# Attention passes: two of a chunk's sixteen gathered columns picked by one-hot fp32 products from a table in SBUF

## The chip, the cores and the metric

The kernel runs on one core of one Trainium2 chip. The metric is the device time of one execution in microseconds, the median of the runs shown.

## What is computed

The reference runs three graph attention layers and one edge MLP over 12,500 nodes with 32 features and 400,000 edges. The edges are sorted by their destination `dst`; `src` is random.

```
def _gat(x, edge_index, W, att_s, att_d, bias, heads, ch, neg_slope):
    h = (x @ W.T).reshape(n, heads, ch)
    a_s = (h * att_s[None]).sum(-1);  a_d = (h * att_d[None]).sum(-1)
    logits = leaky_relu(a_s[src] + a_d[dst], neg_slope)
    m = segment_max(logits, dst);  ex = exp(logits - m[dst])
    denom = segment_sum(ex, dst);  alpha = ex / (denom[dst] + 1e-16)
    return segment_sum(alpha[:, :, None] * h[src], dst).reshape(n, heads * ch) + bias
x = layernorm(x + three_gat_layers(x))
e = relu(concat(x[src], x[dst], edge_attr) @ W1 + b1) @ W2 + b2
x = layernorm(x + maximum(segment_max(e, dst), x))
```

All of it is fp32. The costly part is `h[src]`: for each edge of each layer a row of 32 numbers is fetched from a table of 12,500 rows.

## The kernel before

**Work and tiling.** The 400,000 edges are cut into four quarters of 100,000, and each quarter into 196 chunks of 512 edges (the last two have 352 and 320). A chunk holds 4 x 512 = 2048 edges, laid out as 128 partitions by 16 columns. A pass runs over all 196 chunks. There are three attention passes and one MLP pass, and a node step before each that turns the sums of the pass before into new node features.

**Gathering.** The node step writes `h` for all nodes to `table` in HBM (12,544 rows of 32). For each chunk POOL issues sixteen indirect DMAs, one for each column, in `gather_edges` (L589). Each fetches one row of 32 numbers for each of the 128 partitions, at the indices in `idx`, into a 32-number slot of `g`. There are four `g` and four `idx` buffers, used in turn. The ACT refills `idx` for the chunk four ahead (`refill`) once DVE has read `g`. In the MLP pass the same code fetches rows of 64 numbers from `tablex`.

**One chunk of an attention pass.** DVE's `turn` (L1255) waits for the sixteen gathers and transposes `g` in blocks of 32x32 into `h_sb`, features on the partitions and edges along the free axis. `lead` then scans the destinations' terms forward along the edges (`adf`, L1265). TensorE's `front` computes a restart row (`p_r`, bf16, 4 rows, L676) and spreads the destinations' terms over the partitions (`p_ad`, two fp32 products with 4 rows, L692); `source` makes the attention term of the sources from `h_sb` (`p_as`, L701). DVE's `logits` (L1274 to L1285) forms the logits and their running maximum, ACT's `exps` (L864, L865) the exponentials, and DVE's `sums` (L1292 to L1302) the running sums, which are transposed back and stored to `state` by ACT.

**What sets the order.** Each engine's order is written out by hand. DVE runs `logits(k)`, `lead(k+1)`, `sums(k)`. TensorE runs `front(k)`, `source(k-1)`. ACT runs `exps(k)`, `refill(k+1)`, `restart(k+2)`, `ends_in(k)`, `sloped(k+1)`, `ends_out(k)`. SP loads `ad` and `r_in` two chunks ahead (`load_gat`). POOL issues gathers in chunk order and waits only for `idx`. Semaphores tie them: `tin` counts DVE's transposes, `adf` its scans, `pas` the source products, `e_g` the gathers that landed, `aidx` the index tiles.

**The MLP pass** does two fp32 products of 128 rows on the edge features (L729) and two on the hidden layer (L735), two Relus with a bias column on ACT (L936), and gathers in the same way. `xd_in` holds its destination rows; no attention pass touches it.

Of the kernel before, what the change touches and what calls it, by code (L numbers as in the profile page):

```python
# [19 lines left out]
HID = 64  # L20
# [34 lines left out]
ROUND = float(3 * 2 ** 22)  # L55

# [13 lines left out]
def build(nc, I, out):  # L70
# [3 lines left out]
    with ctx:  # L74
# [11 lines left out]
        def view(t, offset, dims, parts=P, p0=0):  # L86
# [16 lines left out]
        vmax = dram("vmax", (EP, F), fp32)  # L103

# [37 lines left out]
        dt_ = sb("dt_", [HALF, 8, L + 1], i32)  # L142
        rbf = sb("rbf", [HALF, 8, L], bf16)
        row_id = sb("row_id", [P, SAMPLES], i32)
        nodebuf = sb("nodebuf", [P, 2 * TU * L])
# [39 lines left out]
        xd_in = [sb(f"xd_in{b}", [P, W, HID]) for b in range(2)]  # L185
# [3 lines left out]
        hid = d_b  # L189

# [28 lines left out]
        sel_p = [view((xd_in + [dm_t])[t // 8], t % 8 * P, [[1, P]]) for t in range(KT)]  # L219
# [9 lines left out]
        p_t, p_n = bank[0], bank[1:5]  # L229
        p_start, p_next = bank[5][:, 0:NT], bank[5][0:P - 1, P:P + 2]  # L230
# [6 lines left out]
            "l1", "rowi", "bound", "cntv", "sel", "acc", "start", "wpe", "ticks2", "tickl")}  # L237
# [4 lines left out]
            "d", "ph", "s", "ts", "td", "tm", "dm", "st0", "st1")}  # L242
# [41 lines left out]

        def quarters(rows, v):
# [15 lines left out]
        def _(eng):  # L301
# [7 lines left out]
            eng.dma_start(row_id[:, :], I["row_first"].partition_broadcast(P)).then_inc(S["d0"], 16)  # L309

# [71 lines left out]

            head = [eng.value_load(dstp.rearrange("(a b) -> a b", b=1)[LEAD + q * Q:LEAD + q * Q + 1, :], min_val=0, max_val=NP - 1) for q in range(NQ)]
# [3 lines left out]
            def node(step):  # L387
# [24 lines left out]
                if step == 0:  # L412
                    fill_aux()
                    later_inputs()
                    eng.wait_ge(S["rw"], 1)
                    for k in range(8):
                        at = (k % 2) * HALF * NQ * L + (k // 2) * L
                        n = min(HALF, NF - (k % 2) * HALF)
                        eng.dma_start(bass.AP(tensor=rrow.tensor, offset=at, ap=[[NQ * L, n], [1, L]]), rbf[0:n, k, :]).then_inc(S["rw"], 16)
                    for v, at, f, l, n in pieces:  # L420
                        eng.dma_start(bass.AP(tensor=rrow.tensor, offset=v * NQ * L + at, ap=[[NQ * L, 1], [L, NQ], [1, n]]),
                                      view(rbf, L + l, [[2 * L, NQ], [1, n]], parts=1, p0=f - HALF)).then_inc(S["rw"], 16)
                for u in range(NN):
                    eng.wait_ge(n_s[u], (step + 1) * TN * 16)
                for b in range(2):
                    eng.wait_ge(D[f"tst{b}"], TST[b][step + 1])
# [5 lines left out]
            for layer in range(3):  # L432
                node(layer)
                if layer == 0:
                    eng.wait_ge(S["rw"], 1 + 16 * (8 + len(pieces)))
                load_gat(layer, 0, 0)
                load_gat(layer, 1, 1)

                def steps(v, b):
                    if not isinstance(v, int) or v + 2 < NC:  # L440
                        load_gat(layer, v + 2, b)
# [9 lines left out]
                def both(i):  # L451
                    steps(i * 2, 0)
                    steps(i * 2 + 1, 1)
                    fill_x(i)
                both(0)
                with eng.Fori(1, NC // 2 - 2) as i:
                    both(i)
                both(NC // 2 - 2)
                both(NC // 2 - 1)
            node(3)  # L460

            def load_mlp(v, b):
                need(eng, M["pre"], v * 2 - 2)
                tick(eng, "tickl")
                load_r(v, b, M[f"ld{b}"])
                eng.dma_start(chunk_tile(xd_in[b], v, HID), chunk_rows(auxx, v)).then_inc(M[f"ld{b}"], 16)
# [37 lines left out]
        def _(eng):  # L504
            eng.memset(ident[:, :], 0.0).then_inc(S["blk"], 1)
            for o, pattern, base, mult in ((riota, [[BLK, SAMPLES]], 0, 0), (kid_last[:, :], [[BLK * P, KT]], BLK - 1, BLK),
                                           (blk_odd[:, :], [[2 * BLK, NBLK]], -1, 2 * BLK * NBLK), (j_half[:, :], [[1, BLK]], 0, 0),
                                           (kid[:, :], [[P, KT]], 0, 1), (miota[:, :], [[1, P]], 0, 0), (nid[:, :], [[1, NT]], 0, NT)):
# [73 lines left out]
            def gather_edges(pass_, n, k, count=W):  # L582
# [4 lines left out]
                for j in range(count):  # L587
# [24 lines left out]
        def gathered(pass_, i, k, h):  # L612

            last = min(W // 2, max(0, cols(NI - 1, k) // SQ - h * (W // 2))) * 16
            before = pass_ * ((NI - 1) * (W // 2 * 16) + last)
            return before + (NI - 1) * (W // 2 * 16) + last if type(i) is int and i == NI - 1 else i * (W // 2 * 16) + before + W // 2 * 16
# [3 lines left out]
        def _(eng):  # L620
# [57 lines left out]
            for layer in range(3):  # L678
# [23 lines left out]

                front(0, 0)
                front(0, 1)
                source(0, 0)
                for k in range(2, NB):
                    front(0, k)
                    source(0, k - 1)
                with eng.Fori(1, NI - 1) as i:
# [4 lines left out]
                source(NI - 2, NB - 1)  # L714
                for k in range(1, NB):
                    source(NI - 1, k - 1)
                    front(NI - 1, k)
                source(NI - 1, NB - 1)
# [33 lines left out]
        def _(eng):  # L752
# [89 lines left out]
            for layer in range(3):  # L842
# [48 lines left out]

                def chunk(i, k):
                    exps(i, k)
                    if layer or type(i) is not int or i * NB + k > 0:
# [4 lines left out]
                    ends_out(i, k)  # L899
                if layer == 0:  # L900
# [12 lines left out]
                for k in range(NB - 1):  # L913
                    exps(NI - 1, k)
                    ends_in(NI - 1, k)
# [51 lines left out]
        def _(eng):  # L967
# [151 lines left out]
            last.then_inc(S["rw"], 1)  # L1119
            eng.wait_ge(S["par"], N_PAR * 16)  # L1120
# [124 lines left out]
            for layer in range(3):  # L1245
# [3 lines left out]

                def turn(i, k):  # L1250
                    b = k % 2
                    for h in range(2):
# [51 lines left out]
                def chunk(i, k):  # L1304
                    logits(i, k)
                    lead(i if k + 1 < NB else i + 1, (k + 1) % NB)
                    sums(i, k)
                if layer == 0:
                    turn(0, 0)
                    turn(0, 1)  # L1310
# [6 lines left out]
                for k in range(NB - 1):  # L1317
                    logits(NI - 1, k)
                    sums(NI - 1, k)
# [113 lines left out]
```

## Time and profile before

| | |
|---|---|
| median of 3 runs | 16743.22 us (16742.36 to 16745.18) |
| span of the profiled execution | 16709.0 us |
| median of the runs less that span | 34.2 us |
| POOL busy | 12580.8 us (75%) |
| DVE busy | 9733.0 us (58%) |
| TensorE busy (matmul) | 5230.6 us (31%) |
| ACT busy | 2187.6 us (13%) |

The profile shows one execution and gives its span, from the first to the last instruction; a run's time is measured around it, and what lies between the two is launch and end. Busy time is the time in which an engine worked on instructions that the profile counts. A share says little by itself: an engine that starts its next instruction as soon as it can is the bound at 75% too, if the rest is its own issuing.

### The profile page before, as it was taken

How to read it: one execution, taken by the hardware profiler on the slowest of the kernel's cores; microseconds unless marked ns; L12 is line 12 of the kernel's file. 1: busy time of each engine (PE TensorE's matmuls, PEld its weight loads, DVE VectorE, ACT ScalarE, POOL GpSimd, SP SyncE). 2: the span in 40 equal slices, each digit the busy share in tenths (PEclk: the TensorE clock that was granted, in tenths of full speed). 3: DMA queues.
4: the chain of work that ended last, by engine and by line, in shares of the span. 5: the costliest groups of instructions: out<-in, count | busy, mean ns of one | idle time of the engine just before them, and what ended most of it. 6: DMA issues, size and time to landing. Idle time of an engine off the chain costs nothing. (4 is left out here: it accounts for less than half of the span.)

```text
span 16709.0 us, 72365 instructions
## 1 busy us (share of the span) xinstructions
PE 5230.6 (31%) x6238; PEld 1537.5 (9%) x6238; DVE 9733.0 (58%) x11755; ACT 2187.6 (13%) x4747; POOL 12580.8 (75%) x13328
## 2 busy tenths in 40 slices
PE   2333333332233333333223333333323333333332
PEld 1000000000000000000000000000000111111110
DVE  6666666666466666666546666666664444444445
ACT  2111111111011111111101111111111111111110
POOL 7777777777777777777777777777777777777777
PEclk9999999999999999999999999999995666666665
DMA  2111111111011111111101111111112222222222
GB/s 77 58 55 55 56 55 57 55 58 48 20 29 29 29 29 29 29 29 29 28 20 29 29 29 29 28 29 29 29 34 71 79 79 79 79 79 79 79 79 56
DMA packets 639804, 794.40 MB, mean 48 GB/s; under 512 B 252774, under 2 KB 418460, under 8 KB 627084
## 3 DMA queue, kind: packets, MB, share of 16 engines
q0 software_dynamic: 426768, 272.89, 8.8%
q1 hardware_dynamic: 99804, 295.38, 4.8%
q10 hardware_dynamic: 113184, 225.69, 3.7%
q14 instruction: 42, 0.34, 0.0%
q8 instruction: 6, 0.10, 0.0%
HBM read 442.63 MB, written 350.37 MB: 47 GB/s over the span
## 5 line engine op out<-in xcount | busy, mean ns | idle before, releaser
L589 POOL DMA_INDIRECT g<-table,idx x9375 | 8846.2, 944 | 2859.0 <-issue 2856.7
L692 PE MATMUL bank<-ad,ad_sel 4*128 4x512 f32 (+1 forms) x2352 | 2211.4, 1088 | 5306.7 <-DVE adf L1265 5306.7
L589 POOL DMA_INDIRECT g<-tablex,idx x3125 | 2948.4, 943 | 952.4 <-issue 952.4
L1255 DVE STREAM_TRANSPOSE h_sb<-g 128x512 f32<-128x512 f32 (+1 forms) x588 | 606.6, 1032 | 4002.1 <-DMA g<-table,idx 4002.1
L735 PE MATMUL bank<-d_b,w_out 128*128 128x512 f32 (+1 forms) x784 | 727.6, 1083 | 2462.0 <-ACT d_b L936 2462.0
L676 PE MATMUL bank<-r_in,qsel 4*128 4x512 bf16 (+2 forms) x784 | 444.0, 566 | 2875.9 <-issue 1841.0
L1352 DVE STREAM_TRANSPOSE bank<-g 128x512 f32<-128x512 f32 x196 | 142.1, 725 | 1940.8 <-DMA g<-tablex,idx 1940.8
L701 PE MATMUL bank<-h_sb,w_as 128*128 128x512 f32 x1176 | 1216.7, 1139 | 137.5 <-DVE h_sb L1255 137.5
L692 PEld LDWEIGHTS bank<-ad,ad_sel 4*128 4x128 f32 x2352 | 676.0, 316 | 6220.5 <-DVE adf L1265 5603.3
L754 ACT ACTIVATE idx<-idx_all 128x16 int32 (+1 forms) x784 | 168.7, 216 | 6149.2 <-DVE h_sb L1255 3873.2
L1265 DVE TENSOR_TENSOR_SCAN adf<-r_sb,adf,bank 128x512 f32<-128x512 f32 (+1 forms) x588 | 710.2, 1208 | 113.8 <-PE bank L692 113.8
L1281 DVE TENSOR_TENSOR_SCAN mb<-r_sb,mb,xw 128x512 f32<-128x512 f32 (+1 forms) x588 | 751.3, 1278 | 20.7
L1296 DVE TENSOR_TENSOR_SCAN s_b<-pc,s_b,xw 128x512 f32<-128x512 f32 (+1 forms) x588 | 750.4, 1276 | 20.8
L1292 DVE TENSOR_TENSOR_SCAN d_b<-pc,d_b,xw 128x512 f32<-128x512 f32 (+1 forms) x588 | 728.2, 1238 | 12.1 <-ACT pc L865 12.1
L1285 DVE TENSOR_TENSOR xw<-xw,mb 128x1024 f32<-128x1024 f32 (+1 forms) x588 | 721.9, 1228 | 20.1
L754 ACT ACTIVATE r_sb<-bank 128x512 f32<-128x512 f32 (+2 forms) x784 | 466.7, 595 | 1547.2 <-DVE s_b L1360 1111.7
L864 ACT ACTIVATE xw<-xw 128x512 f32<-128x512 f32 (+1 forms) x588 | 341.3, 580 | 2387.1 <-DVE xw L1285 2387.1
L1278 DVE TENSOR_TENSOR xw<-u_sb,xw 128x512 f32<-128x512 f32 (+1 forms) x588 | 408.2, 694 | 355.9 <-ACT u_sb L872 355.9
L1298 DVE STREAM_TRANSPOSE dm_t<-d_b 128x512 f32<-128x512 f32 (+1 forms) x588 | 592.3, 1007 | 0.0
L754 ACT ACTIVATE o_sb<-dm_t 128x64 f32<-128x64 f32 (+1 forms) x588 | 181.5, 309 | 3076.5 <-DVE dm_t L1299 3076.5
L1302 DVE STREAM_TRANSPOSE o_sb<-s_b 128x512 f32<-128x512 f32 (+1 forms) x588 | 581.4, 989 | 0.0
L1299 DVE STREAM_TRANSPOSE dm_t<-mb 128x512 f32<-128x512 f32 (+1 forms) x588 | 580.1, 987 | 0.0
(225 smaller groups left out, 7127.5 us busy)
## 6 DMA issues: line engine op xcount, KB each, us to landing
state<-o_sb ACTq DMA_DIRECT2D x582, 288.0 KB, 2.1
g<-table,idx POOLq DMA_INDIRECT x9375, 2.3
auxx<-wide SPq DMA_DIRECT2D x97, 1056.0 KB, 4.2
xd_in<-auxx SPq DMA_DIRECT2D x194, 512.0 KB
xe_t<-in_edge_attr SPq DMA_DIRECT2D x196, 256.0 KB
g<-tablex,idx POOLq DMA_INDIRECT x3125, 2.4
vmax<-o_sb ACTq DMA_DIRECT2D x194, 256.0 KB, 2.1
r_in<-rrow SPq DMA_DIRECT2D x776, 4.0 KB
```

Of the source, the lines that this page charges most:

```text
L589: eng.indirect_dma_start(o, None, t[:, :], bass.IndirectOffsetOnAxis(ap=idx[k][:, j:j + 1], axis=0)).then_inc(e_g[k][j // (W // 2)], 16)
L692: last = eng.matmul(p_ad[:, 0:c], ad_sel[:, h, :], view(ad[b], h, [[2, c]], parts=NQ), start=(h == 0), stop=(h == 1))
L701: eng.matmul(p_as[:, 0:c], w_as[layer][:, :], h_sb[b][:, 0:c], start=True, stop=True).then_inc(E["pas"], 1)
L735: last = eng.matmul(p_v[:, 0:cols(v)], w_out[:, h, :], hid[h][:, 0:cols(v)], start=(h == 0), stop=(h == 1))
L754: return eng.activation(o, i, ACT.Copy)
L1255: v_.transpose(view(h_sb[b], 0, [[1, w], [w, SQ]]), view(g[k], 0, [[F, w], [1, F]])).then_inc(E["tin"], 1)
L1265: v_.tensor_tensor_scan(adf[b][:, 0:c], r_sb[b][:, 0:c], p_ad[:, 0:c], adf[1 - b][:, e - 1:e], ALU.min, ALU.max).then_inc(E["adf"], 1)
L1281: v_.tensor_tensor_scan(mb[b][:, 1:c + 1], r_sb[b][:, 0:c], xw[:, 0, 0:c], mb[b][:, 0:1], ALU.min, ALU.max).then_inc(E["mb"], 1)
L1285: v_.tensor_tensor(xw[:, :, 0:c], xw[:, :, 0:c], view(mb[b], 1, [[0, 2], [1, c]]), ALU.subtract).then_inc(E["dif"], 1)
L1292: v_.tensor_tensor_scan(d_b[b][:, 0:c], pc[:, 0:c], xw[:, 0, 0:c], d_b[1 - b][:, e - 1:e], ALU.mult, ALU.add).then_inc(E["d"], 1)
L1296: v_.tensor_tensor_scan(s_b[b][:, 0:c], pc[:, 0:c], xw[:, 0, 0:c], s_b[1 - b][:, e - 1:e], ALU.mult, ALU.add).then_inc(E["s"], 1)
L1298: v_.transpose(dm_t[:, 0, 0:w, :], view(d_b[b], 0, [[1, w], [w, SQ]])).then_inc(E["td"], 1)
```

## The change

In the attention passes, columns 0 and 1 of each chunk are no longer gathered (`SEL = 2`); columns 2 to 15 are. The MLP pass still gathers all sixteen.

Node `n` of the table is written as `n = 98 p + 14 b + t`, with partition `p` (the *key*, 0 to 127), block `b` (0 to 6) and place `t` (0 to 13). At the start of each pass SP loads the whole table into `h_all` (an idle part of `nodebuf`, 12,544 rows, node `98 p + s` on partition `p`), and ACT reorders it into `by_place`, seven blocks of 32 features by 14 places, 448 numbers for each partition. Once, at the start of the kernel, DVE splits the source index of the selected edges into `key = floor(n / 14)` (that is `7 p + b`), and `t` and `t * t` (`digits`), and SP writes them to HBM as `keys` and `digit`.

For each chunk and each pass:

- SP loads the chunk's 256 keys, broadcast to 128 partitions (`kb`, two buffers), and three rows of 256 (one, t, t squared; `ms`, four buffers).
- ACT makes seven one-hot matrices `oh` of 128x256 (one buffer): seven Squares of (key - own key), then one Relu of 1 - 2 x that over all 1792 columns.
- TensorE, for each of the two columns, adds into one PSUM bank of 128x448 (`p_sel`, banks 4 and 5) one product with 3 rows (`ms` by `mcoef`), which is zero at the wanted place and at most -2^118 elsewhere, and seven products with 128 rows (`oh` by `by_place`). All are fp32.
- DVE takes the maximum over the 14 places for each feature, which leaves the wanted row, and writes it into `g` where the gather used to.

The orders become: DVE `logits(k)`, `lead(k+1)`, `picked(k+2)`, `sums(k)`; TensorE `front(k)`, `source(k-1)`, `select(k+1)`; ACT `exps(k)`, `one_hot(k+3)`, then as before; SP `load_gat(k+2)`, `load_sel(k+3)`. Some tiles that are idle in the attention passes are shared (`oh` with `xd_in`, `by_place` and `ms` with the setup's tiles).

```diff
@@ gather_edges (POOL)
-                for j in range(count):
+                for j in range(SEL if pass_ < 3 else 0, count):
...
@@ block.sync
+            def load_sel(layer, x, k):
+                n = layer * NC + x
+                need(eng, E["far"], n - 1)
+                tick(eng, "tickl")
+                need(eng, E["sel"], n - 3)
...
+                eng.dma_start(kb[k % 2], row.partition_broadcast(P)).then_inc(E[f"lk{k % 2}"], 16)
+                eng.dma_start(ms[k], cols_).then_inc(E[f"lk{k % 2}"], 16)
...
+                    eng.dma_start(h_all, table.rearrange("(p t) c -> p (t c)", t=NT)).then_inc(E["href"], 16)
+                    for x in range(3):
+                        load_sel(step, x, x)
...
@@ block.tensor
+                def select(i, k):
+                    n = i * NB + (layer * NC + k)
+                    need(eng, E["oh"], n + 1)
+                    for c in range(SEL):
+                        at = slice(c * P, (c + 1) * P)
+                        need(eng, E["red"], n * SEL + (c + 1 - SEL))
+                        eng.matmul(p_sel[c][:, 0:FT], ms[k][:, at], mcoef[:, :], start=True, stop=False)
+                        for b in range(NN):
+                            last = eng.matmul(p_sel[c][:, 0:FT], oh[:, b, at], by_place[:, b, :], start=False, stop=(b == NN - 1))
+                    last.then_inc(E["sel"], 1)
...
                 with eng.Fori(1, NI - 1) as i:
                     for k in range(NB):
                         front(i, k)
                         source(i - (k == 0), (k - 1) % NB)
+                        select(i if k + 1 < NB else i + 1, (k + 1) % NB)
...
@@ block.scalar
+                def halves():
+                    eng.wait_ge(E["href"], (layer + 1) * 16)
+                    for b in range(NN):
+                        last = copy(by_place[:, b, :].rearrange("p (f t) -> p f t", f=F), view(nodebuf, b * FT, [[1, F], [F, TN]]))
+                    last.then_inc(E["by"], 1)
+
+                def one_hot(i, k):
+                    x = i * NB + k
+                    n = x + layer * NC
+                    need(eng, E[f"lk{k % 2}"], (x - k % 2) * 16 + (layer * NC * 16 + 32))
+                    tick(eng, "ticks")
+                    need(eng, E["oh"], n)
+                    tick(eng, "ticks")
+                    need(eng, E["sel"], n)
+                    for b in range(NN):
+                        last = eng.activation(oh[:, b, :], kb[k % 2], ACT.Square, scale=-1.0, bias=key_at[:, b:b + 1])
+                    last.then_inc(E["far"], 1)
+                    need(eng, E["far"], n + 1)
+                    eng.activation(oh[:, :, :], oh[:, :, :], ACT.Relu, scale=-2.0, bias=1.0).then_inc(E["oh"], 1)
+
                 def chunk(i, k):
                     exps(i, k)
+                    one_hot(i if k + 3 < NB else i + 1, (k + 3) % NB)
...
@@ block.vector
+                def picked(i, k):
+                    n = i * NB + (layer * NC + k)
+                    need(eng, E["sel"], n + 1)
+                    for c in range(SEL):
+                        v_.tensor_reduce(view(g[k], c * F, [[1, F]]), view(p_sel[c], 0, [[TN, F], [1, TN]]), AX.X, ALU.max).then_inc(E["red"], 1)
+
                 def turn(i, k):
                     b = k % 2
+                    n = i * NB + (layer * NC + k)
+                    need(eng, E["red"], n * SEL + SEL)
...
                 def chunk(i, k):
                     logits(i, k)
                     lead(i if k + 1 < NB else i + 1, (k + 1) % NB)
+                    picked(i if k + 2 < NB else i + 1, (k + 2) % NB)
                     sums(i, k)
```

## Rows read from the trace of the kernel before

**Rows 1.** The page: busy time by engine; granted clock in 40 slices, in tenths.

```profile
PE 5230.6 (31%) x6238; PEld 1537.5 (9%) x6238; DVE 9733.0 (58%) x11755; ACT 2187.6 (13%) x4747; POOL 12580.8 (75%) x13328
...
PEclk9999999999999999999999999999995666666665
```

**Rows 2.** The page, costliest groups: out<-in, count | busy, mean ns | idle, releaser.

```profile
L589 POOL DMA_INDIRECT g<-table,idx x9375 | 8846.2, 944 | 2859.0 <-issue 2856.7
...
L1255 DVE STREAM_TRANSPOSE h_sb<-g 128x512 f32<-128x512 f32 (+1 forms) x588 | 606.6, 1032 | 4002.1 <-DMA g<-table,idx 4002.1
```

**Rows 3.** Timeline of one attention chunk: start, duration, engine, line, operation [idle before].

```profile
2001.42 1.04 DVE L1255 STREAM_TRANSPOSE h_sb<-g 128x512 f32<-128x512 f32 x1 [6.63 <-DMA g<-table,idx]
...
2003.45 1.24 DVE L1292 TENSOR_TENSOR_SCAN d_b<-pc,d_b,xw 128x512 f32<-128x512 f32 x1
...
2003.58 3.78 PE L692 MATMUL bank<-ad,ad_sel 4*128 4x512 f32 x4 [9.34 <-DVE adf L1265]
...
2007.29 2.08 PE L701 MATMUL bank<-h_sb,w_as 128*128 128x512 f32 x2
...
2009.43 0.67 DVE L1274 TENSOR_TENSOR xw<-adf,bank 128x512 f32<-128x512 f32 x1
...
2013.54 1.23 DVE L1285 TENSOR_TENSOR xw<-xw,mb 128x1024 f32<-128x1024 f32 x1
...
2014.80 0.58 ACT L864 ACTIVATE xw<-xw 128x512 f32<-128x512 f32 x1 [4.07 <-DVE xw L1285]
...
2015.29 0.59 ACT L865 ACTIVATE pc<-xw 128x512 f32<-128x512 f32 x1
...
2021.42 1.04 DVE L1255 STREAM_TRANSPOSE h_sb<-g 128x512 f32<-128x512 f32 x1 [6.65 <-DMA g<-table,idx]
```

**Rows 4.** Timeline of TensorE, two chunks of the MLP pass, and one weight load.

```profile
12704.46 3.78 PE L735 MATMUL bank<-d_b,w_out 128*128 128x512 f32 x4 [12.89 <-ACT d_b L936]
...
12709.02 1.98 PE L729 MATMUL bank<-xe_t,w_hid 128*128 128x512 f32 x4 [0.27 <-DVE pc L1342]
12709.61 0.19 PEld L729 LDWEIGHTS bank<-xe_t,w_hid 128*128 128x128 f32 x1 [0.30 <-DVE mb L1342]
...
12724.35 3.78 PE L735 MATMUL bank<-d_b,w_out 128*128 128x512 f32 x4 [13.35 <-ACT d_b L936]
...
12728.91 3.75 PE L729 MATMUL bank<-xe_t,w_hid 128*128 128x512 f32 x4 [0.25 <-DVE pc L1342]
```

**Rows 5.** Windows in these chunks: stretch, length, busy by engine, granted clock, DMA, GB/s.

```profile
12708.00:12709.00 1.00, 0.75 (x2) 0.10 (x1) 1.00 (x3) 0.00 (x0) 0.95 (x1) 0.70 0.17 33
12709.00:12710.00 1.00, 0.98 (x3) 0.50 (x4) 1.00 (x2) 0.00 (x0) 0.72 (x1) 1.00 0.14 33
...
12715.00:12716.00 1.00, 0.00 (x0) 0.00 (x0) 0.00 (x0) 0.00 (x0) 0.69 (x2) 0.71 0.05 10
...
12732.50:12733.00 0.50, 0.16 (x1) 0.00 (x0) 0.00 (x0) 0.00 (x0) 0.20 (x1) 1.00 0.97 393
...
12735.50:12736.00 0.50, 0.00 (x0) 0.00 (x0) 0.00 (x0) 0.00 (x0) 0.50 (x1) 0.91 0.09 29
```

**Rows 6.** Timeline of ACT in the MLP pass.

```profile
13023.25 0.69 ACT L936 ACTIVATE d_b<-bank,b_hid 128x512 f32<-128x512 f32 x1 [0.26 <-DVE bank L1356]
13023.85 0.69 ACT L936 ACTIVATE d_b<-xw,b_hid 128x512 f32<-128x512 f32 x1
```

**Rows 7.** Groups by line and shape: Sign, table load and reduction (last of the third node step).

```profile
L764 ACT ACTIVATE x_nm<-nodebuf,bound 128x512 f32<-128x512 int32 x49 | 35.4, 722 | 1.6
...
L764 ACT ACTIVATE x_nm<-row_id,blk_odd 128x784 f32<-128x784 int32 x14 | 13.3, 949 | 0.4
...
L822 ACT ACT_TABLE_LOAD x7 | 9.0, 1283 | 0.1
...
L1235 DVE TENSOR_REDUCE row<-nodebuf 128x14 f32<-128x448 f32 x7 | 4.3, 620 | 0.2
```

**Rows 8.** The page, DMA issues: out<-in, engine, count, KB, us to landing.

```profile
auxx<-wide SPq DMA_DIRECT2D x97, 1056.0 KB, 4.2
```

More of the change, by code:

```diff
@@ L55 @@
 ROUND = float(3 * 2 ** 22)
+SEL = 2
+FT = F * TN
+SPLIT = NT * F
+FAR = float(2 ** 118)
+NKEY = NC * SEL
 def first(v):
@@ L103, in build @@
         vmax = dram("vmax", (EP, F), fp32)
+        keys = dram("keys", (NC, SEL * P), fp32)
+        digit = dram("digit", (3, NC * SEL * P), fp32)
         ident = sb("ident", [P, P])
@@ L184, in build @@
         gx = g
-        xd_in = [sb(f"xd_in{b}", [P, W, HID]) for b in range(2)]
+        xd2 = sb("xd2", [P, 2, W, HID])
+        xd_in = [xd2[:, b, :, :] for b in range(2)]
         xds = [[adf[b], h_sb[b]] for b in range(2)]
@@ L189, in build @@
         hid = d_b
+        oh = view(xd2, 0, [[SEL * P, NN], [1, SEL * P]])
+        h_all = nodebuf[:, 0:NT * F]
+        src_key = mb[0][:, 0:NKEY].bitcast(i32)
+        key = xe_t[0][:, 0:NKEY]
+        digits = [xe_t[1][:, 0:NKEY], view(x1_nm, 0, [[1, NKEY]])]
+        ones = view(o_sb[0], 0, [[1, NKEY]])
+        place14 = view(o_sb[1], 0, [[1, FT]], parts=3)
+        place_sq = view(o_sb[0], 0, [[1, FT]], parts=3)
+        place_c = view(o_sb[1], FT, [[1, 1]], parts=3)
         ends = sb("ends", [P, 3, OW])
@@ L449, in fill_x, with four @@
                                       wide[:, 0:min(w, total - i * w) if isinstance(i, int) else w]).then_inc(S["wide"], 16)
[L451 to L459, printed above, removed]
+                def four(i):
+                    for k in range(NB):
+                        steps(i * NB + k, k)
+                        if k % 2:
+                            fill_x(i * 2 + k // 2)
+                four(0)
+                with eng.Fori(1, NI - 1) as i:
+                    four(i)
+                four(NI - 1)
             node(3)
@@ L612, in gathered @@
         def gathered(pass_, i, k, h):
-            last = min(W // 2, max(0, cols(NI - 1, k) // SQ - h * (W // 2))) * 16
-            before = pass_ * ((NI - 1) * (W // 2 * 16) + last)
-            return before + (NI - 1) * (W // 2 * 16) + last if type(i) is int and i == NI - 1 else i * (W // 2 * 16) + before + W // 2 * 16
+            skip = lambda p: SEL if p < 3 and h == 0 else 0
+            each = lambda p: (W // 2 - skip(p)) * 16
+            last = lambda p: (min(W // 2, max(0, cols(NI - 1, k) // SQ - h * (W // 2))) - skip(p)) * 16
+            before = sum((NI - 1) * each(p) + last(p) for p in range(pass_))
+            if type(i) is int and i == NI - 1:
+                return before + (NI - 1) * each(pass_) + last(pass_)
+            return i * each(pass_) + (before + each(pass_))
         @block.tensor
@@ L705, in _ @@
                 source(0, 0)
+                select(0, 2)
                 for k in range(2, NB):
@@ L708, in _ @@
                     source(0, k - 1)
+                    select(0 if k + 1 < NB else 1, (k + 1) % NB)
                 with eng.Fori(1, NI - 1) as i:
@@ L717, in _ @@
                     front(NI - 1, k)
+                    if k + 1 < NB:
+                        select(NI - 1, k + 1)
                 source(NI - 1, NB - 1)
@@ L899, in chunk @@
                     ends_out(i, k)
+                halves()
+                for k in range(3):
+                    one_hot(0, k)
                 if layer == 0:
@@ L1306, in chunk @@
                     lead(i if k + 1 < NB else i + 1, (k + 1) % NB)
+                    picked(i if k + 2 < NB else i + 1, (k + 2) % NB)
                     sums(i, k)
                 if layer == 0:
-                    turn(0, 0)
-                    turn(0, 1)
+                    place_rows()
+                for k in range(2):
+                    picked(0, k)
+                    if layer == 0:
+                        turn(0, k)
                 lead(0, 0)
@@ L1424 @@
     arrays, aps = {}, {}
-    for name in _INS + ["x_t", "row_first"]:
+    for name in _INS + ["x_t", "row_first", "src_key"]:
         a = np.ascontiguousarray(laid[name])
```

79 lines of the change are left out of this document (65 added, 14 removed), and 2 rows, old and new, of the table E.

## The prediction

> **What bounds the kernel now.** I read the page's busy shares first [rows 1]. POOL holds 75% and no other engine passes 58%, so I ask whether POOL ever waits. The costliest groups answer it: the 9,375 gathers of the attention passes cost 944 ns each, with 2859.0 us of idle time between them, 2856.7 of it put down to "issue" and not to another engine [rows 2]. That is 305 ns each, and one gather takes 1.249 us; POOL starts the next as soon as it can. The same rows show DVE idle for 4002.1 us, waiting for gathered data. The timeline of one chunk says where: the transpose of the gathered tile starts at 2001.42 and again at 2021.42, after an idle 6.65 us that a gather ended [rows 3]. So the 588 attention chunks (3 passes of 196) are paced by POOL: 16 gathers, 19.98 us a chunk.
>
> **What is removed.** Two gathers per chunk, 2 x 588 = 1176. At 1.249 us that is 1468 us, and a chunk of 14 gathers costs POOL 17.48 us. Nothing hides this work, so all of it is won if every other loop closes in under 17.48 us. Such a loop decides.
>
> **What is added on TensorE.** Per chunk two selects, each 1 product with 3 rows and 7 with 128 rows, fp32, 448 columns. The trace shows an fp32 product as two records: the two products of L692 are x4, 3.78 us [rows 3], the same as the two of L735 [rows 4], that is about 0.85 us a record of 512 columns and a tail. In the MLP pass a burst of four records takes 3.78 us before the granted clock has risen and 1.98 us where it is 1.00 [rows 4, 5]. [...]
>
> **Which level.** In the MLP pass the clock rose near 12708.6, after L735 had run from 12704.46, and in the next chunk near 12732.5, after L735 and L729 from 12724.35: 4.1 and 8.1 us of nearly unbroken products [rows 4, 5]. [...] It fell near 12715.5 and 12735.9, that is 4.5 and 3.2 us after the last product ended [rows 4, 5]. In between, the products of 12709 to 12711 held it. What the added gap between two selects does is open, and is the main doubt below.
>
> **What is added on ACT.** Per chunk 7 Squares of 128x256 and one Relu of 128x1792. None stands in the trace. Nearest are the two Relus with a bias column of L936: 0.69 us each, 0.60 us start to start at 512 elements [rows 6]; Sign takes 722 ns at 512 and 949 at 784, or 0.83 ns an element [rows 7]. A Square of 256 then starts 0.39 us after the last, the seventh takes 0.47: 2.8 us. The Relu is 0.69 + 1280 x 0.00083 = 1.75 us, and the waits before, between and after cost 0.2 us, three at the 0.06 us that passes between the end of L701 and L1274 behind it [rows 3]. Sum 4.75 us. From below, with spacing as for the two Exps of L864 and L865 (0.49 us at 512, [rows 3]) it is 4.0; from above, each Square whole (0.47 us), 5.4.
>
> **The loop that decides.** There is one `oh`. The ACT writes it for chunk n+1 only when the select of chunk n is done, and the next select waits for that. So select and one-hot follow each other strictly: 12.2 + 4.75 = 16.95 us a chunk (bounds 16.1 and 17.7). That is 0.5 us under POOL's 17.48. In the gap TensorE does its old products (about 3 us), which need only the scan of L1265, finished earlier. While ACT waits for the select, the copies and exponentials queued behind it wait too; exps(n) stand ahead of it, and DVE's use of the later ones comes after the gap.
>
> **DVE.** Two max-reductions of 128x448 from PSUM. L1235 reduces 448 elements to 14 in 620 ns [rows 7]; from PSUM I allow 0.55 to 0.75 each, 1.3 us with the hand-over. Transpose to scan 2.03 us, sums 5.98, logits 5.34 [rows 3]: 13.35 + 1.3 = 14.7 us a chunk, 2.8 under 17.48. Hidden; without cover it would be 1.3 x 588 = 765 us.
>
> **SP and DMA.** Two more loads a chunk, into double and fourfold tiles, requested two to three chunks ahead; SP issues four loads a chunk instead of two. Zero; above, if they landed late, the select would slip by some 2 us.
>
> **Edges.** [...] Bounds 0 and 20 us a pass, taken 8: 25 us. The setup's few extra operations on DVE and POOL lie beside searches and scatters: 0.
>
> **The sum.** Against the profiled span: 16709.0 - 1468 + 25 = 15,266 us. The runs' median of 16743.2 lies 34.2 us above that span, outside it, unchanged: 15,300. For a loop nearer its upper end (17.7, then 0.2 x 588 = 130 us, at two chances in five) I add 50: **15,350 us**, 8.3% less. The best is 15,270.
>
> [...]
>
> **Rivals.** First, *the clock falls in the gap*. From the end of a select to the full-row part of the next there are 4.75 us and 0.75 of a 3-row product, in which only the source product (0.85 us) has 128 rows. For it: L692 with 4 rows and L701 keep TensorE busy 5.8 us a chunk and never bring the clock up, so 4-row products seem to count for little, and 3.2 to 4.5 us without products sufficed for a fall [rows 3 to 5]. Against it: the gap isn't idle, and what sufficed there was wholly idle time. A fall costs half of the 4.1 to 8.1 us at the slow level, 2 to 4 us. If some two in three gaps bring one, the loop is 16.95 + 0.66 x 3.05 = 19.0 us; 588 x (19.98 - 19.0) = 576, so 16,170 us; falls of one in three, 18.0 us, 15,600. [...]
>
> Second, and slower, *a fall in every gap*, with the one-hot leg at 4.75 or more: 12.2 + 3.6 + 4.75 = 20.55 us a chunk, over POOL's 19.98. Then 588 x 0.57 = 335 us lost, 17,080. It decides from a loop of 19.98 on, that is a fall in each chunk costing more than 3.0 us. Same rows for and against; it needs the gap to count as idle always.
>
> Third, *loads*: a load of 0.19 us not hidden before each of 32 records makes 18.3 + 4.75 = 23 us, 18,500 us. Fourth, *never fast*: 24.1 + 4.75 = 28.9 us, 21,960 us; against both stand the rows of the MLP pass. Fifth, Square could bring a table load (1283 ns, [rows 7]) twice a chunk, 19.5 us, 16,470; Copy, Exp, Relu and Sign change places without one in the trace.
>
> **How the numbers follow.** Forecast (POOL paces, clock holds or falls seldom) 0.52, own range 15,260 to 15,600. Clock falls in part of the gaps 0.30 (15,600 to 16,700). Fall in every gap 0.11. Loads 0.02, never fast 0.02, table load 0.03. The range 15,260 to 16,700 holds the first two, the table load and little of the third: about 0.84. A difference of under 0.2% (33 us) can't be told from none. Slower: 0.10 + 0.04 and 0.01 of the second case's top, 0.15; same 0.03; faster 0.82.
>
> **What would show it.** L589 at 8,199 gathers of table, 944 ns, still behind "issue" alone; if it waits for an ACT index copy or DVE transpose, the loop is longer than 17.48. DVE's transpose waiting for the gather, not its new reduction for TensorE. The select's 32 records in 12.2 us, the one-hot in 4.75 us, starting within 0.1 us of the select's end. The granted clock near 1.0 with records of 0.375 us confirms the level; falls show as records of 0.75 us. Wrong it is if records stay at 0.75 us, or if the chunk is above 18 us.

## The result, and the profile after

| | before | after |
|---|---|---|
| median | 16743.8 us | 17145.5 us |
| ratio, 95% interval | | 1.024 (1.0225 to 1.0254) |
| span of the profiled execution | 16709.0 us | 17143.7 us |
| gathers of `table` | 9375 | 8199 |

The kernel is slower by 402 us, outside the forecast range. The 34.2 us between the median and the span of the kernel before are not launch and end, as was written ahead of the prediction: the runs of the kernel after lie 1.9 to 2.1 us above their own spans, and the kernel before took 16,711 to 16,731 us in the experiments below. The profiled execution was one of that kind. Beside such a time (16712.5 us) the same loop took 17145.9 us (the run with POOL's work given back), 433 us more; that is the size to compare with the spans. Why the kernel before took 16,743 us in the table isn't known.

The page of the kernel after, with busy time, granted clock in tenths and the costliest groups (these answer to [rows 1, 2]):

```profile
PE 12607.5 (74%) x25054; PEld 5123.9 (30%) x25054; DVE 10375.5 (61%) x12943; ACT 4808.5 (28%) x9472; POOL 11501.1 (67%) x12154
...
PEclk6888888887688888888768888888875666666665
...
L645 POOL DMA_INDIRECT g<-table,idx x8199 | 7755.4, 946 | 4157.8 <-issue 2433.9
L771 PE MATMUL bank<-early,xd 128*128 128x448 f32 x16464 | 7657.6, 625 | 0.0
...
L1383 DVE TENSOR_REDUCE g<-bank 128x32 f32<-128x448 f32 x1176 | 679.8, 620 | 3697.7 <-PE bank L771 3697.7
L988 ACT ACTIVATE xd<-row_id,key_at 128x256 f32<-128x256 f32 x4116 | 1706.2, 494 | 4117.0 <-PE bank L771 4117.0
```

The waits of POOL (waiting line, released by: us in total, times, longest):

```profile
POOL g L645 <- issue: 3386.8, 10777, 1.3
POOL g L645 <- ACT idx L835: 1721.7, 546, 26.8
```

POOL, which waited for nobody before, now stands 1721.7 us behind the index copies of ACT. DVE's 4002.1 us of waiting for gathered data [rows 2] have shrunk to 143.0; in their place DVE's new reduction waits 3697.7 us for TensorE, and ACT's Squares 4117.0 us for TensorE. POOL's gathers still cost 946 ns. The bound has moved to the loop of select and one-hot.

One chunk of it, the timeline of the kernel after (start, duration, engine, line):

```profile
2003.31 1.85 PE L769 MATMUL bank<-early 3*128 3x448 f32 x2 [1.63 <-ACT xd L991]
...
2005.09 7.49 PE L771 MATMUL bank<-early,xd 128*128 128x448 f32 x14
...
2012.51 1.01 PE L769 MATMUL bank<-early 3*128 3x448 f32 x2
...
2013.46 5.53 PE L771 MATMUL bank<-early,xd 128*128 128x448 f32 x14
...
2018.92 0.38 PE L736 MATMUL bank<-r_in,qsel 4*128 4x512 bf16 x1
...
2019.02 2.90 ACT L988 ACTIVATE xd<-row_id,key_at 128x256 f32<-128x256 f32 x7 [6.93 <-PE bank L771]
2019.14 1.96 PE L752 MATMUL bank<-ad,ad_sel 4*128 4x512 f32 x4
...
2021.03 1.12 PE L761 MATMUL bank<-h_sb,w_as 128*128 128x512 f32 x2
...
2021.95 1.70 ACT L991 ACTIVATE xd<-xd 128x1792 f32<-128x1792 f32 x1
...
2023.78 1.85 PE L769 MATMUL bank<-early 3*128 3x448 f32 x2 [1.63 <-ACT xd L991]
```

And the granted clock in it, from windows (stretch, length, busy by engine with count, granted clock, DMA, GB/s; these answer to [rows 5]):

```profile
2008.00:2009.00 1.00, 1.00 (x3) 0.35 (x2) 0.97 (x1) 0.00 (x0) 0.76 (x1) 0.50 0.27 76
2010.00:2011.00 1.00, 1.00 (x4) 0.46 (x3) 1.00 (x2) 0.00 (x0) 0.70 (x2) 1.00 0.10 16
...
2021.00:2022.00 1.00, 1.00 (x3) 0.30 (x2) 0.97 (x2) 0.97 (x4) 0.27 (x1) 1.00 0.06 6
2022.00:2023.00 1.00, 0.15 (x1) 0.00 (x0) 0.96 (x2) 1.00 (x1) 0.00 (x0) 0.87 0.13 31
2023.00:2024.00 1.00, 0.22 (x1) 0.23 (x2) 1.00 (x2) 1.00 (x3) 0.00 (x0) 0.50 0.21 58
```

The loop closes in the rows: first column 2003.31 to 2012.51, 9.20 us, begun at a granted clock of 0.50 (the slow level); second column to 2018.99, 6.48 us, at 1.00 (the fast level); then the gap to 2023.78, 4.79 us, in which ACT writes the one-hot. The sum is 20.47 us, one chunk. The clock falls in the gap, 0.6 us after the source product ended and 3.8 us after the last product of the select (0.87 granted in the stretch from 2022 puts it near 2022.74). Counted in the trace, between 700 and 3500 us the clock fell 137 times in 136 chunks, each time from 1.00 to 0.50. Each time it stays at the slow level for 6.8 us, most of it over the first column of the next select. It costs 9.20 - 6.48 = 2.7 us a chunk. Without it the chunk would be 17.75 us, still a little over POOL's 17.48.

Where the 434.7 us between the spans lie: the three attention passes, from first to last scan of `adf`, took 3812.6, 3882.3 and 3882.2 us before and 4003.2, 4002.3 and 4002.1 after, 430.5 us more. The pace is 298 of it: 588 x 0.507 us, from 19.97 us a chunk before and 20.48 after. Some 62 us are the ends of the passes, 21 each. The third and second last steps between scans take 35.6 and 27.6 us where they took 20.5 and 15.5, since DVE's order for the last chunks of a pass puts `picked` and `sums` ahead of the next `lead`, and TensorE waits for the transpose in it:

```profile
4204.75 5.53 PE L771 MATMUL bank<-early,xd 128*128 128x448 f32 x14
4218.45 2.07 PE L761 MATMUL bank<-h_sb,w_as 128*128 128x512 f32 x2 [8.17 <-DVE h_sb L1392]
```

The start of the second and third pass costs nothing (17.5 and 18.5 us for the first steps, against 20.1 and 19.9). About 70 us more lie in the first pass: its first steps took 13.3 us before, while four chunks gathered ahead lasted, and take 20.5 to 20.7 after, from the third on. That lead saves nothing once POOL isn't the bound.

### The profile page after: what moved, and what is told of

It reads as the page before. It is cut to its first block and busy times, and to the rows that moved or that the text cites. A ratio compares the mean times of both kernels' runs of the same rounds, so it can differ in the third digit from the quotient of the medians.

```text
span 17143.7 us, 121556 instructions
## 1 busy us (share of the span) xinstructions
PE 12607.5 (74%) x25054; PEld 5123.9 (30%) x25054; DVE 10375.5 (61%) x12943; ACT 4808.5 (28%) x9472; POOL 11501.1 (67%) x12154
## 5 line engine op out<-in xcount | busy, mean ns | idle before, releaser
L645 POOL DMA_INDIRECT g<-table,idx x8199 | 7755.4, 946 | 4157.8 <-issue 2433.9
L771 PE MATMUL bank<-early,xd 128*128 128x448 f32 x16464 | 7657.6, 625 | 0.0
L771 PEld LDWEIGHTS bank<-early,xd 128*128 128x128 f32 x16464 | 3527.7, 221 | 4423.4 <-issue 4423.4
L1383 DVE TENSOR_REDUCE g<-bank 128x32 f32<-128x448 f32 x1176 | 679.8, 620 | 3697.7 <-PE bank L771 3697.7
L988 ACT ACTIVATE xd<-row_id,key_at 128x256 f32<-128x256 f32 x4116 | 1706.2, 494 | 4117.0 <-PE bank L771 4117.0
L769 PE MATMUL bank<-early 3*128 3x448 f32 x2352 | 1684.1, 806 | 1014.2 <-ACT xd L991 1014.2
L752 PE MATMUL bank<-ad,ad_sel 4*128 4x512 f32 (+1 forms) x2352 | 1164.5, 613 | 19.7 <-DVE adf L1402 19.7
L769 PEld LDWEIGHTS bank<-early 3*128 3x128 f32 x2352 | 463.7, 244 | 1880.3 <-issue 1834.7
L991 ACT ACTIVATE xd<-xd 128x1792 f32<-128x1792 f32 x588 | 997.6, 1697 | 18.6
L1418 DVE TENSOR_TENSOR_SCAN mb<-r_sb,mb,xw 128x512 f32<-128x512 f32 (+1 forms) x588 | 751.2, 1278 | 20.7
L1422 DVE TENSOR_TENSOR xw<-xw,mb 128x1024 f32<-128x1024 f32 (+1 forms) x588 | 722.4, 1229 | 20.1
L761 PE MATMUL bank<-h_sb,w_as 128*128 128x512 f32 x1176 | 669.3, 651 | 71.3 <-DVE h_sb L1392 71.3
```

What stands on the lines that cost most here:

```text
L645: eng.indirect_dma_start(o, None, t[:, :], bass.IndirectOffsetOnAxis(ap=idx[k][:, j:j + 1], axis=0)).then_inc(e_g[k][j // (W // 2)], 16)
L752: last = eng.matmul(p_ad[:, 0:c], ad_sel[:, h, :], view(ad[b], h, [[2, c]], parts=NQ), start=(h == 0), stop=(h == 1))
L769: eng.matmul(p_sel[c][:, 0:FT], ms[k][:, at], mcoef[:, :], start=True, stop=False)
L771: last = eng.matmul(p_sel[c][:, 0:FT], oh[:, b, at], by_place[:, b, :], start=False, stop=(b == NN - 1))
L988: last = eng.activation(oh[:, b, :], kb[k % 2], ACT.Square, scale=-1.0, bias=key_at[:, b:b + 1])
L991: eng.activation(oh[:, :, :], oh[:, :, :], ACT.Relu, scale=-2.0, bias=1.0).then_inc(E["oh"], 1)
```

## The experiments

Every run was timed beside the kernel before on the same chip, which took 16,712 to 16,729 us there. The pace of a chunk below is the spacing of the scans of `adf` in the trace, and "falls" are counted in its record of the clock, both between 700 and 3500 us. No run shows a clock in GHz: the fast level of the expectations is a granted clock of 1.00, the slow one of 0.50.

**The removal alone.** The kernel before with `for j in range(2 if pass_ < 3 else 0, count)` in `gather_edges`, and the counts that are waited for lowered to match. It leaves two of sixteen source rows out of the computation.

> The kernel before, gathering only columns 2 to 15 in the attention passes; the two others keep what is in the tile, so two of sixteen source rows are left out of the computation. This is the removal alone. Forecast's removal term: 1468 us less, 15,275 us, chunk 17.48 us, POOL behind issue alone. Rival, that another loop (DVE 13.4 us and its waits) shows below 19.98: over 15,400 us.

Measured 15279.1 us, chunk 17.48 us. DVE keeps up. The kernel before took 16712.5 us beside it, so what the change takes away is worth 1,433 us and not 1,468. That the time itself came out within 4 us of 15,275 is luck: the 16,743 us that it was reckoned from was 31 us too high for this comparison. The 35 us lie where POOL doesn't pace: the last three steps of a pass took the same 20.5, 15.4 and 11.7 us with and without the two gathers, and so did the first ten of the first pass (12.4 to 13.4 us).

**POOL given its work back.** The kernel after, with the selected columns gathered as well:

```diff
-                for j in range(SEL if pass_ < 3 else 0, count):
-                    o, t = (g[k][:, j // 2, ...], table)
+                for j in range(count):
+                    o, t = (spill[:, k, j, :] if j < SEL else g[k][:, j // 2, ...], table)
...
```

> The changed kernel, and POOL gathers all sixteen columns again, the two selected ones into a tile that nothing reads. If the loop of select and one-hot paces the chunk (20.48 us against POOL's 19.98 for 16 gathers), the 1176 gathers put back cost next to nothing: 17,146 to 17,250 us. If POOL had a part in the 20.48 us, they cost up to 1468 us: up to 18,610 us.

Measured 17145.9 us, the same as without them. 1176 gathers are free there: POOL has no part in the 20.48 us.

**The gap filled, with 128 rows and with 4.** Two products ahead of the wait for the one-hot, into the bank that the select overwrites:

```diff
                 def select(i, k):
                     n = i * NB + (layer * NC + k)
+                    need(eng, E["red"], n * SEL + (1 - SEL))
+                    for _ in range(2):
+                        eng.matmul(p_sel[0][:, 0:FT], w_as[layer][:, :], by_place[:, 0, :], start=True, stop=True)
                     need(eng, E["oh"], n + 1)
```

and the same with `ad_sel[:, 0, :]` and `by_place[0:NQ, 0, :]`, 4 rows each.

> The changed kernel, and TensorE does two more fp32 products of 128 rows by 448 columns (a constant by by_place, into a bank that the next select overwrites) before it waits for the one-hot. Clock theory: the clock falls once a chunk because the gap between two selects holds too few 128-row products; the four extra records (1.5 us at 2.4 GHz) lie in the 1.63 us in which TensorE is idle, the granted clock stays at 1.00, all select records take 0.375 us, the loop is about 17.0 us and POOL's 17.48 us paces the chunk: 17,146 - 588 x 3.0 = 15,380 us. Rival, that the clock only follows and the leg over ACT and the semaphores is what is long: chunk 20.5 to 22 us, 17,150 to 18,000 us.

> As the run with two added 128-row products, but the two added products have 4 rows, and so the same length on TensorE. Clock theory with rows (few-row products don't hold the clock): it still falls once a chunk, the chunk stays at 20.5 us or a little more, 17,150 to 17,400 us. Rival, that any product holds the clock and only the 1.63 us of idle time lets it fall: as fast as with 128 rows, about 15,380 us.

With 128 rows 15868.7 us, with 4 rows 17564.3 us. The groups of both in the same stretch of 1000 us, 128 rows first:

```profile
L645 POOL DMA_INDIRECT g<-table,idx x765 | 721.8, 943 | 279.5 <-issue 237.8 <-ACT idx L838 41.8
L774 PE MATMUL bank<-early,xd 128*128 128x448 f32 x1525 | 620.2, 559 | 0.0
...
L767 PE MATMUL bank<-early,w_as 128*128 128x448 f32 x217 | 110.8, 641 | 0.0
```

```profile
L645 POOL DMA_INDIRECT g<-table,idx x659 | 621.7, 943 | 379.2 <-issue 195.7 <-ACT idx L838 183.5
L774 PE MATMUL bank<-early,xd 128*128 128x448 f32 x1316 | 621.3, 632 | 0.0
...
L767 PE MATMUL bank<-early,ad_sel 4*128 4x448 f32 x192 | 122.7, 775 | 0.0
```

The added instructions are as many and TensorE has next to no idle time left in either (998.2 and 1000.0 us busy in 1000); 14 gathers a chunk give 18.3 us (765 gathers) and 21.2 us (659). The clock fell 43 times in 153 chunks with 128 rows and in each chunk with 4. So it is neither idle time by itself nor ACT's leg: the 4-row products didn't hold the clock where 128-row products did, and the falls cost what was missing. Zeros in an operand aren't the reason: the one-hot matrices are nearly all zeros, and in the kernel after the clock rises in every chunk while the select reads them (0.50 granted in the stretch from 2008, 1.00 in that from 2010). The run with 4 rows is slower than its expectation allowed (17,400 us): its four added records take 775 ns each, 3.1 us, and don't fit in the 1.63 us of idle time. Adding 128-row work to the critical engine made the kernel 1,277 us faster. It is short of the 15,380 expected: chunks without a fall took 17.60 us, just over POOL's, so no fall was made good later.

**One column instead of two** (`SEL = 1`).

> SEL = 1: one column picked, fifteen gathered. POOL needs 15 x 1.249 = 18.73 us a chunk. [...] The loop is at most 15.3 us, under POOL's, so what the clock does should not matter: 588 gathers less, 734 us less than before, and up to 20 us a pass of edges: 16,010 to 16,070 us (against 16,743). If the added work costs by itself, not through the loop, the gain is smaller.

Measured 16025.7 us, 689 us less than the 16714.7 beside it; chunk 18.73 us, POOL's pace exactly. The clock was at the slow level for 64% of the time and cost the pace nothing: the loop has slack. No run shows the terms behind its bound of 15.3 us, a select wholly at the slow level above all: in the chunk at 2001.33 the select took 10.1 us, with the clock at 1.00 from 2009 on, and the one-hot behind it 3.1.

**3-row products moved into the gap.** Nothing added:

```diff
+                    need(eng, E[f"lk{k % 2}"], (i * NB + k - k % 2) * 16 + (layer * NC * 16 + 32))
...
+                    for c in range(SEL):
+                        at = slice(c * P, (c + 1) * P)
+                        need(eng, E["red"], n * SEL + (c + 1 - SEL))
+                        eng.matmul(p_sel[c][:, 0:FT], ms[k][:, at], mcoef[:, :], start=True, stop=False)
                     need(eng, E["oh"], n + 1)
...
```

> The changed kernel with the two 3-row products of a chunk issued ahead of the wait for the one-hot, so that they lie in the gap. Nothing is added. Loop theory: the part of the select behind the one-hot falls from 12.8 to about 11.2 us at 2.4 GHz, the clock still falls once a chunk since 3-row products don't hold it, so the chunk is 20.48 - 1.6 = 18.9 us and the time 16,200 us. Rival, that any products in the gap hold the clock: 17.48 us by POOL, 15,320 us. Rival, that the chunk is tied to the times at which the clock changes: it stays at 20.48 us, 17,146 us.

Measured 16224.3 us (two runs, 16183.5 and 16265.1), chunk 18.95 us in the mean; single chunks from 15.6 to 20.6 us. In the mean the loop is additive: 1.6 us out of it, 1.5 us gained, at the same time at the slow level (6.9 us a chunk here, 6.8 in the kernel after). Single chunks aren't: the commonest (68 of 147) is 20.6 us long, and 15.6 us ones follow it. The mean isn't tied to the times at which the clock changes. The two runs lie 0.5% apart, more than those of any other kernel here.

**Both at once.**

> The two added 128-row products and the 3-row products ahead of the wait for the one-hot. The gap then holds some 5.8 us of products against a one-hot leg of 4.8 us, so TensorE is never idle and paces the chunk: 15.6 + 1.5 + small waits, 17.2 to 17.6 us if the clock holds: 15,300 to 15,450 us. If the stretch of few-row products (3.2 us now instead of 1.7) lets the clock fall more often than in the run with two 128-row products alone (0.28 falls a chunk): over 15,870 us.

Measured 15373.7 us, 5 falls in 162 chunks, POOL at 802 gathers in 1000 us, its full pace. The windows of this run, its clock ahead of DMA share and GB/s:

```profile
1000.00:2000.00 1000.00, 1000.00 (x2504) 450.21 (x2503) 796.38 (x932) 420.20 (x819) 755.86 (x802) 0.99 0.24 71
2000.00:3000.00 1000.00, 999.47 (x2495) 449.23 (x2494) 794.03 (x929) 416.51 (x813) 755.87 (x802) 0.99 0.24 71
```

**The loop cut by a second one-hot tile**, in an idle part of `nodebuf`:

```diff
-        oh = view(xd2, 0, [[SEL * P, NN], [1, SEL * P]])
+        oh = [view(xd2, 0, ...), view(nodebuf, 2 * TU * L - NN * SEL * P, ...)]
...
-                    need(eng, E["sel"], n)
+                    need(eng, E["sel"], n - 1)
...
```

TensorE and ACT then use `oh[k % 2]`.

> The changed kernel with two one-hot tiles (the second in an idle part of nodebuf), so that ACT writes one while TensorE reads the other. The loop of select and one-hot is cut, but TensorE still has its 4-row products between two selects. If the loop was the cause and the clock holds (no wait is left in the gap): POOL paces, 17.48 us, 15,320 us. If few-row products let the clock fall all the same: TensorE needs 15.6 us at the fast level and 2 to 3.5 us more for a fall a chunk, 17.6 to 19.1 us, 15,400 to 16,250 us. If the loop didn't matter: 17,146 us.

Measured 15825.9 us. TensorE has no wait at all, yet the clock fell in 143 of 153 chunks:

```profile
2000.00:3000.00 1000.00, 1000.00 (x2144) 418.20 (x2145) 748.63 (x879) 390.38 (x770) 726.23 (x770) 0.88 0.23 68
```

TensorE is busy for all of the 1000 us, at 0.88 granted. A chunk takes 18.2 us, of which 16.0 us are the products, as the quickest chunk shows. Here, being always busy did not hold the clock.

**Two tiles and the two added products.**

> Two one-hot tiles and two added 128-row products before each select. The loop is cut and TensorE has 17.1 us of products a chunk at the fast level, 1.5 of them added. Clock theory: the few-row stretch (restart, the 4-row products, 2.1 us) is followed by 128-row products only, the clock holds, TensorE or POOL paces at 17.1 to 17.5 us: 15,300 to 15,400 us, though there is more work than in the run with two one-hot tiles (15,826 us). Rival, that the added work costs what it takes: 15,826 + 588 x 1.5 = 16,700 us.

Measured 15789.7 us, a miss. The clock fell in 36 of 154 chunks, and chunks without a fall took 17.48 us: the added work had used up the slack that would have made the falls good.

**Few-row products spread.** Two tiles; L752's products stand between the two columns.

```diff
                     for c in range(SEL):
+                        if c and between:
+                            spread(*between)
...
```

> Two one-hot tiles, and the two 4-row products of L752 moved between the two columns of a select; no product is added. Clock theory (long stretches of few-row products and idle time let it fall): what stood in one stretch of 2.7 us or more is now cut into two of under 2 us each, the clock holds in nearly all chunks, TensorE needs 15.6 us and small waits, POOL paces at 17.48: 15,300 to 15,400 us. If only the share of few-row products and idle time counts and not where they stand: as with two one-hot tiles alone (0.93 falls a chunk), 15,826 us.

Measured 15761.9 us, a miss: 139 falls in 154 chunks. The timeline shows why the spreading did little:

```profile
2003.58 2.06 PE L759 MATMUL bank<-ad,ad_sel 4*128 4x512 f32 x4
2005.48 0.91 PE L778 MATMUL bank<-early 3*128 3x448 f32 x2
2006.32 7.23 PE L780 MATMUL bank<-early,xd 128*128 128x448 f32 x14
```

The 4-row products now touch the second column's 3-row product: 2.7 us of few-row work in one piece, and after it 7.23 us for what takes 5.53 at the fast level.

**The 3-row product put inside the column**, with and without the spreading.

```diff
-                        eng.matmul(p_sel[c][:, 0:FT], ms[k][:, at], mcoef[:, :], start=True, stop=False)
                         for b in range(NN):
+                            if b == 4:
+                                eng.matmul(p_sel[c][:, 0:FT], ms[k][:, at], mcoef[:, :], start=False, stop=False)
+                            last = eng.matmul(p_sel[c][:, 0:FT], ..., start=(b == 0), stop=(b == NN - 1))
```

> As the run with two one-hot tiles and the 4-row products between the columns, and each column's 3-row product stands behind its fourth 128-row product instead of ahead of the first. No product is added or left out. In that run 4-row and 3-row products stood together for 2.7 us; here no stretch of few-row products is over 1.9 us and each has 128-row products on both sides, as in the run at 17.1 us a chunk with 3-row products ahead of the wait. Theory of the unbroken stretch: the clock holds, TensorE needs 16.0 us, POOL paces: 15,290 to 15,400 us. Rival, that the share of few-row products counts wherever they stand, and only added 128-row products cure it: 15,762 us as there.

> As the run with two one-hot tiles (15,826 us, 0.93 falls a chunk), with each column's 3-row product behind its fourth 128-row product; the 4-row products stay ahead of the source product. Theory of the unbroken stretch: the longest is the restart, what idle time POOL leaves, and the 4-row products, 1.9 us of products and up to 1.5 idle; falls only where the idle time is long, so POOL's pace is kept: 15,290 to 15,450 us. Rival as for the other run: 15,826 us.

Measured 15351.1 us with the spreading (ratio 0.9185, 0.917 to 0.9201) and 15350.5 us without (0.9185, 0.9169 to 0.92). Against the runs with the 3-row product in front, one instruction in each column has changed its place, and that is worth 411 and 475 us. (The 411 are between runs on two chips, whose kernel before took 16,729 and 16,713 us; the 475 are on one chip.) The move saves no product time: a chunk wholly at the fast level takes 15.98 us in both runs without the spreading, and 16.37 us against 15.98 with it. The first of the two:

```profile
L645 POOL DMA_INDIRECT g<-table,idx x802 | 756.7, 944 | 244.4 <-issue 244.4
...
2000.00:3000.00 1000.00, 976.20 (x2237) 392.61 (x2237) 786.95 (x921) 405.06 (x800) 755.91 (x802) 0.97 0.24 70
```

POOL is back behind "issue" alone. With the spreading the clock fell 45 times in 161 chunks, against 139 in 154 with the same products in the other order: where the products stand counts, and their share isn't all that counts. Without the spreading the time was met, but not for the reason given. The clock was to fall only where idle time was long. It fell 102 times in 162 chunks though TensorE was busy for 99 to 100% of the time, 92 of these times in the 4-row products or the source product right behind them. It came back sooner than in the run with two tiles alone (2.34 us a chunk at the slow level, not 4.55), and at 16.0 us for a chunk without a fall TensorE makes up for it. Both are faster than either kernel, by 8% than the one before, and 72 us from the removal alone.

**What a fall costs.** In four runs TensorE has next to no wait and POOL has slack. There a chunk, counted from one restart row to the next on TensorE, takes what its products take at the fast level, and half of its time at the slow level on top:

| run | chunk wholly at the fast level, us | time at the slow level a chunk, us | first and half of the second | mean chunk, us |
|---|---|---|---|---|
| two 128-row products added | 17.60 | 1.45 | 18.3 | 18.27 |
| two tiles | 15.98 | 4.55 | 18.3 | 18.21 |
| two tiles and two products | 17.48 | 1.27 | 18.1 | 18.10 |
| two tiles, spread | 15.98 | 4.12 | 18.0 | 18.11 |

So the falls are all that these runs miss, and the run with the 3-row product inside the column (15.98 and 2.34) stays under POOL's 17.48.

## Why the prediction was wrong

- **The removal** (1468 us, 17.48 us a chunk) was right in the pace, which is 17.48 us, and 35 us too large in the sum: 1,433 us in the run of the removal alone.
- **The loop that decides** was the right loop: the one-hot leg was put at 4.75 us and measured 4.79. The select at the fast level was put at 12.2 us, and no run shows that term: it is 2 x 6.48 = 12.95 at a granted clock of 1.00, since a gap of 0.2 us behind each 3-row product (2012.51 to 2013.46 for its two records) and the hand-overs were missing. Nor does a run show the 24.1 us of a select wholly at the slow level: in the rows above it was at 1.00 within 7 us of its start. The old products, put at about 3 us, took 3.2 (2018.92 to 2022.15); the 3-row and the source product in the gap, put at 0.75 and 0.85 us, stand in the rows with 1.01 and 1.12. So even with a steady clock the loop has 17.6 to 17.75 us, over POOL's 17.48 and not 0.5 under it, as the run with 128-row filling shows (17.60).
- **The time of a record** was right. The source product L701 is one and stands as x2, 2.08 us, the two of L692 as x4, 3.78 us [rows 3]: two records more for 1.70 us, 0.85 each and 0.38 beyond them. By columns that is 0.75 us at 448, and half of it 0.375. The weight loads of the select in the kernel after, one ahead of each record, start 0.75 us apart where the granted clock is 0.50 and 0.37 to 0.38 where it is 1.00:

```profile
2006.00 0.34 PEld L771 LDWEIGHTS bank<-early,xd 128*128 128x128 f32 x1 [0.41 <-issue]
2006.75 0.34 PEld L771 LDWEIGHTS bank<-early,xd 128*128 128x128 f32 x1 [0.41 <-issue]
...
2009.79 0.19 PEld L771 LDWEIGHTS bank<-early,xd 128*128 128x128 f32 x1 [0.19 <-issue]
2010.16 0.19 PEld L771 LDWEIGHTS bank<-early,xd 128*128 128x128 f32 x1 [0.19 <-issue]
```

- **"Which level"** is the step that failed. It took the select to be at the fast level for most of its length, which it is, and left open what the gap does, with 0.52 on "holds or falls seldom" and 0.11 on a fall in every gap. It falls in every gap, 137 times in 136 chunks, and so the loop takes 20.48 us and paces, not POOL. The size of a fall lay in the range: 2.7 us measured, 2 to 4 expected. That the second rival's chunk was 20.55 us where 20.48 was measured is partly luck: it put the fall at 3.6 us, 0.9 too much, and the select at 12.2, 0.75 too little. What told against a fall, that the gap isn't wholly idle, was worth nothing: the run with 4-row filling shows that such products did not hold the clock. The rows had hinted at it: L692 and L701 keep TensorE busy 5.8 us and never raise the clock (the four records of L692 take 3.78 us, as those of L735 do at the slow level [rows 3, 4]), while in the MLP pass it rose 4.1 us after L735 began [rows 4, 5].
- **"The clock holds and few falls are absorbed"** also needed slack, and by the sizes above there was none. The three runs with two columns at POOL's pace had it: 17.1 us of products with 5 falls, 16.4 with 45, and 16.0 with 102. Of the two misses, the run with two tiles and two products had none (17.48 us without a fall). The spread one had 1.5 us (16.0 without a fall), and falls in 139 of 154 chunks cost it more than that, 2.1 us in the mean.
- **Edges** were put at 25 us, a term that no run shows, and are some 137, what is left of 434.7 after the pace: 21 us a pass instead of 8, and at the pass's end, not at its start where they were looked for; 70 us from the lead of four chunks in the first pass, which was not seen; and 4 outside the passes. **The 34.2 us** added for what lies outside the span are 1.9 to 2.1 in the kernel after, and at most 2.4 in any run that lists both times. In the run of the removal alone, paced by POOL, the first pass still is 58 us shorter than the second; at POOL's pace the best runs lie 72 us above the removal alone.
- **DVE** was right: 620 ns a reduction, hidden. **Loads** were right: the weight loads are hidden, 14 records at a granted clock of 1.00 taking 5.53 us, 14 x 0.375 and 0.28, with a load of 0.15 to 0.19 us before each. No table load was added (x7 and x6 in both kernels). **The one-hot leg's** upper bound was added up 0.1 us too high (5.4 for 5.3), which changes nothing.

Open: what makes the clock fall. The run with both changes in the gap has 5 falls in 162 chunks and the one with two tiles and filling 36 in 154, with the same added products in another order; no run here tells what makes that difference. The theory of the unbroken stretch, which the last runs were built on, does not settle it. The restart row and the 4-row products stand together for 2.1 us in the run with two tiles (143 falls in 153 chunks), in that with the 3-row product inside the column (102 in 162), and in the two just named (36 and 5). What a bf16 one-hot would do was not tried.

## What to carry to other kernels

Price a new TensorE job at both clock levels (0.75 and 0.375 us a record here) and ask of each stretch between its dense products how many rows the products there have, not only whether the engine is busy. With 3- and 4-row products touching the clock fell in 139 of 154 chunks; with the 3-row product moved among 128-row products, in 45 of 161. Such a move is cheap to try and, by these runs, hard to forecast. Where two engines hand one buffer to and fro, add both sides and the gap before comparing with the engine that paces; a forecast with 0.5 us of slack in a chunk of 17 is a coin toss. Take an idle engine's share from the pacing one only as far as that closed loop allows: here one column was safe at once, two only once the clock was kept up for most of the time, with the loop cut or with products moved into its gap.

## What the runs showed of the hardware

- Adding two fp32 products of 128 rows to the pacing engine made the kernel faster (17,146 to 15,869 us), adding two of 4 rows slower (17,564 us).
- The granted clock fell from 1.00 to 0.50 while TensorE was 100% busy (run with two tiles: mean clock 0.88, 1000.00 us busy in 1000).
- The granted clock is printed as 9 to 10 tenths in passes where the products took the slow level's time (L692 3.78 us [rows 1, 3]; the same four records, L752 in the kernel after, 1.96 us at 1.00). Executions of this same kernel within 3 us of each other (16710.6 to 16713.8) are listed with a mean clock of 0.90 or of 0.53. Up to the first change of level in the traces of this kernel, the duration of a product says more than the column.
- Where TensorE paced, a chunk took its products' time at a granted clock of 1.00 and half of what it spent at 0.50 (18.27, 18.21, 18.10 and 18.11 us in four runs, to 0.1).
- Moving one instruction within each accumulation changed the time by 3% (15,826 to 15,351 us).
